# State-space decays from cumulative sums spread over partitions through DRAM and subtracted on GpSimd, experts taken in pairs, rotation prepared in halves

## The reference, cut to what matters

```python
dt = jax.nn.softplus(dt_raw + dt_bias)
a = jnp.exp(-jnp.exp(A_log) * dt)
Bh = jnp.repeat(_rms(Braw), HEADS_PER_GROUP, axis=2) + B_bias
Ch = jnp.repeat(_rms(Craw), HEADS_PER_GROUP, axis=2) + C_bias
phi = jnp.cumsum(dt, axis=1)[..., None] * rope_freqs
Bh = _rope(Bh, phi)
Ch = _rope(Ch, phi)
u = xh * dt[..., None]
...
h = a_t[..., None, None] * h + u_t[..., None] * b_t[:, :, None, :]
y = jnp.einsum('bhpn,bhn->bhp', h, c_t)
```

```python
hid = x @ w1[e].T            # 352 wide: gate and up
act = weight[:, e] * silu(hid[:, :176]) * hid[:, 176:]
y += act @ w2[e].T
```

## Time and profile before

| | us |
|---|---|
| median of 3 runs | 3548.45 (3546.27 to 3550.61) |
| the profiled execution's own time | 3546.08 |
| its span | 3543.8 |
| state-space loop, one pass (window 1244.60 to 1302.90) | 58.30 |
| DVE busy in that pass | 50.68 |
| PE busy in that pass | 46.95 |
| POOL busy in that pass | 13.82 |

### The profile page before, as it was taken

One profiled execution on the slowest core, in us unless ns is written; L12 is line 12 of the kernel. 1 busy time (PEld: TensorE's weight loads), 2 busy tenths in 40 slices (PEclk: granted clock), 3 DMA queues, 4 the chain that ended last, 5 costly groups with the idle time before them and its releaser, 6 DMA issues. The chain is left out here.

```text
span 3543.8 us, 63690 instructions
## 1 busy us (share of the span) xinstructions
PE 2886.8 (81%) x24052; PEld 2012.8 (57%) x24052; DVE 2235.7 (63%) x4757; ACT 1481.2 (42%) x3064; POOL 628.6 (18%) x990
## 2 busy tenths in 40 slices
PE   6777699977767878848996958979999996888687
PEld 3333488867645555525664434536565565777576
DVE  6999644432658888866655733257777774433764
ACT  4899511111454646343442122245555541332222
POOL 5222100000002222111110014112222212322100
PEclk8899799989977776769998978989999997999798
DMA  4999900000010000010001050000000003000000
GB/s 122 199 204 205 225 4 0 0 24 3 17 54 3 3 2 3 2 73 10 6 12 50 23 143 24 0 7 4 3 3 3 3 3 148 1 1 1 1 1 13
DMA packets 316791, 141.92 MB, mean 40 GB/s; under 512 B 296251, under 2 KB 306107, under 8 KB 312897
## 3 DMA queue, kind: packets, MB, share of 16 engines
q1 hardware_dynamic: 308356, 138.85, 16.4%
q10 hardware_dynamic: 8256, 0.52, 0.2%
HBM read 68.04 MB, written 3.15 MB: 20 GB/s over the span
## 5 line engine op out<-in xcount | busy, mean ns | idle before, releaser
L1251 ACT ACTIVATE l0x_pb<-l0x_ex,l0x_neg_max,l0x_q_scale 128x2048 uint16<-128x2048 f32 x128 | 267.2, 2088 | 35.3 <-POOL l0x_neg_max L1354 24.8
L1150 PE MATMUL l0x_s_ps<-l0x_kT,l0x_qT 128*128 128x512 bf16 x512 | 178.3, 440 | 78.8 <-DVE l0x_ex L1449 42.1
L1447 DVE TENSOR_SCALAR_CACHE_REDUCE l0x_ex<-l0x_s_ps 128x1024 f32<-128x1024 f32 x128 | 156.1, 1220 | 13.6 <-PE l0x_s_ps L1150 12.8
L1449 DVE TENSOR_SCALAR_CACHE_REDUCE l0x_ex<-l0x_s_ps 128x1024 f32<-128x1024 f32 x128 | 156.1, 1219 | 1.0 <-PE l0x_s_ps L1150 1.0
L1150 PEld LDWEIGHTS l0x_s_ps<-l0x_kT,l0x_qT 128*128 128x128 bf16 x512 | 33.5, 101 | 157.7 <-DVE l0x_ex L1449 106.3
L264 PE MATMUL l3x_bank<-l3x_w_kv_x,l3x_ctxT 128*128 128x512 f32 x256 | 117.4, 601 | 4.4 <-ACT l3x_ctx_q L765 3.7
L2230 PE MATMUL l1a_bank<-l1a_r,l1a_r 32*64 32x64 f32 x2048 | 73.1, 285 | 44.6 <-DVE l1a_r L2572 40.1
L2238 PEld LDWEIGHTS l1a_bank<-l1a_u,l1a_gm 64*64 64x64 f32 x2048 | 97.7, 197 | 17.8 <-issue 17.0
L2238 PE MATMUL l1a_bank<-l1a_u,l1a_gm 64*64 64x8 f32 x2048 | 100.4, 237 | 7.5 <-DVE l1a_gm L2591 7.3
L264 PE MATMUL l2f_bank<-l2f_w,l2f_ln_yT 128*128 128x352 f32 x256 | 105.6, 548 | 0.0
L1160 PEld LDWEIGHTS l0x_o_ps<-l0x_v,l0x_vT 128*128 128x128 f16 x2048 | 71.6, 99 | 56.5 <-DMA l0x_vT<-l0x_pb 26.7
(11 more groups left out here) (775 smaller groups left out, 7690.5 us busy)
## 6 DMA issues: line engine op xcount, KB each, us to landing
l2f_wproj_raw<-in_L_xattn_wproj SPq DMA_DIRECT2D x2, 2048.0 KB, 13.4
l3a_w<-in_L_attn_W SPq DMA_DIRECT2D x4, 1024.0 KB, 11.8
l2f_w<-in_L_ffn_w SPq DMA_DIRECT2D x1, 2816.0 KB, 10.7
l0x_ex<-in_ctxT SPq DMA_DIRECT2D x8, 256.0 KB, 5.3
l0a_wq<-in_L_attn_W_Q SPq DMA_DIRECT2D x1, 2048.0 KB, 11.4
l0a_wk<-in_L_attn_W_K SPq DMA_DIRECT2D x1, 2048.0 KB, 14.2
l0x_vT<-l0x_pb SPq DMA_TRANSPOSE x128, 4.7
l0a_wv<-in_L_attn_W_V SPq DMA_DIRECT2D x1, 2048.0 KB, 8.0
```

Source lines behind the costliest of these rows:

```text
L1150: ins = mm(s_ps[:, j * 512:(j + 1) * 512], qT[:, h, :], kT[:, h // 2, j * 512:(j + 1) * 512], start=True, stop=True)
L1251: s.activation(pb[:, h % 4, :], ex[:, h % 4, :], ACT.Exp, scale=q_scale[:, h:h + 1], bias=nb[:, h:h + 1], accum_out=sums[:, h:h + 1]).then ...
L1447: v.tensor_scalar(ex[:, h % 4, 0:1024], s_ps[:, 0:1024], 1.0, None, ALU.mult, ALU.max, accum_out=low_max[:, h:h + 1]).then_inc(o.up(scores ...
L1449: v.tensor_scalar(ex[:, h % 4, 1024:2048], s_ps[:, 1024:2048], 1.0, None, ALU.mult, ALU.max, accum_out=high_max[:, h:h + 1]).then_inc(o.up ...
```

## The change

In the state-space part:

- The running sums are also copied times -exp(A_log) to cum_a (ACT, heads on partitions), stored in DRAM, and read back eight times a tile, each time 16 heads of one sequence broadcast to the 64 partitions of that sequence, straight into the decay tile (8 transfers of 64 x 4 KB). PE turns cum_a once, ACT copies it to cum_s, tokens on partitions.
- POOL subtracts cum_s and adds a mask, in place, two instructions of 128x1024 for each of the four rounds (function differences). ACT takes the exponential in place from SBUF.
- The step tiles, their instructions on DVE and POOL, and the matmuls 2218 and 2219 go. So do the DVE instruction for dt times a and the setup of the two masks.
- The bias of the B states is added by POOL alone, in four instructions of 128x1024, the first half of head groups first.
- On ACT the bias of C and the sines go by halves: bias, sines, bias, sines.

In the expert part two experts share one activation tile of 352 columns, which is transposed in three pieces (128, 128, 96) and multiplied in three matmuls, in place of two and two for each expert. The second weight matrix is laid out for that.

```diff
+            for t in range(TILES):
+                sp.wait_ge(cum_a_ready.sem, cum_a_ready.value(t))
+                sp.dma_start(cum_dram[t].rearrange("b h s -> h b s"), cum_a[0:H, :].rearrange("h (b s) -> h b s", b=2)).then_inc(cum_stored.sem, 16)
+                sp.wait_ge(cum_stored.sem, cum_stored.value(t))
+                for r in range(4):
+                    if t and r % 2 == 0:
+                        sp.wait_ge(gm_ready.sem, gm_ready.value(t - 1, r // 2 + 1))
+                    for b in range(2):
+                        src = cum_dram[t, b, 16 * r:16 * r + 16, :].unsqueeze(0).broadcast_to([S, 16, S])
+                        sp.dma_start(decay[b * S:(b + 1) * S, 16 * r:16 * r + 16, :], src).then_inc(spread_loaded[r].sem, 16)
...
-            def differences(t, r):
-                steps_ready = (even_steps, odd_steps)[r % 2]
...
-                    mm(bank[4 + j][:], later[:].rearrange("p b s -> p (b s)"), same[:].rearrange("p h s -> p (h s)"), start=True, stop=False)
-                    ins = mm(bank[4 + j][:], after[:], flat(steps_[:, 8 * j:8 * j + 8, :]), start=False, stop=True)
...
+            def turn_sums(t):
+                pe.wait_ge(cum_a_ready.sem, cum_a_ready.value(t))
+                pe.sem_inc(L.order["pe"], 1)
+                nc.tensor.transpose(cum_s_bank, cum_a[0:H, :], env.ident[0:H, 0:H]).then_inc(cum_s_ps.sem, 1)
...
+                s.activation(cum_a[:], bank[2][:, 256:384], ACT.Copy, scale=a_neg[:]).then_inc(o.up(cum_a_ready), 1)
...
             def decays(o, r):
-                act.wait_ge(diff_ps.sem, diff_ps.value(o.t, r + 1))
-                for j in range(2):
-                    h = 16 * r + 8 * j
-                    s.activation(flat(decay[:, h:h + 8, :]), bank[4 + j][:], ACT.Exp).then_inc(o.up(exp_ready if j else None), 1)
+                act.wait_ge(diff_ready.sem, diff_ready.value(o.t, r + 1))
+                d = flat(decay[:, 16 * r:16 * r + 16, :])
+                s.activation(d, d, ACT.Exp).then_inc(o.up(exp_ready), 1)
...
+                    act.wait_ge(roped.sem, roped.value(t, 1))
+                    biased_c(o, 0)
+                    sums_out(o)
+                    sines(o, 0)
                     act.wait_ge(roped.sem, roped.value(t))
-                    biased_c(o)
-                    sines(o)
+                    biased_c(o, 1)
+                    sines(o, 1)
...
+            def differences(o, r):
+
+                heads = slice(16 * r, 16 * r + 16)
+                d = decay[:, heads, :]
+                pool.wait_ge(spread_loaded[r].sem, spread_loaded[r].value(o.t))
+                pool.wait_ge(cum_s_ready.sem, cum_s_ready.value(o.t))
+                g_.tensor_tensor(d, d, cum_s[:, heads].unsqueeze(2).broadcast_to([P, 16, S]), ALU.subtract).then_inc(o.up(), 1)
+                pool.wait_ge(o.sem, o.at())
+                g_.tensor_tensor(d, d, mask[:].unsqueeze(1).broadcast_to([P, 16, S]), ALU.add).then_inc(o.up(diff_ready), 1)
...
-                steps_of(o, 2)
...
-                    steps_of(o, 0)
-                    biased_b(o)
                     fractions(o)
...
+                for n, (a, w) in enumerate(self.parts):
+                    ins = nc.tensor.matmul(self.y, self.actT[0:w, pair % 2, n, :], self.w_out[0:w, pair, n, :],
+                                           start=(pair == 0 and n == 0), stop=(2 * pair == E - 2 and n == len(self.parts) - 1))
```

More of the change, by code:

```diff
@@ L599, in __init__ @@
         self.fixed, self.factor = fixed, factor
-        self.parts = [(a, min(P, inner - a)) for a in range(0, inner, P)]
+        self.parts = [(a, min(P, 2 * inner - a)) for a in range(0, 2 * inner, P)]
         self.score = L.sb(f"{name}_score", [P, 8])
@@ L665, in scalar @@
                 s.activation(self.sg[:, i % 2, :], self.hb[i % 2][:, 0:I], ACT.Silu).then_inc(o.up(self.silu), 1)
[L666 to L671, removed]
+            if i >= 2 and i % 2 == 0:
+                pair = i // 2 - 1
+                o.eng.wait_ge(self.actT_ps.sem, self.actT_ps.value(o.t, pair + 1))
+                whole_rows = len(self.parts) - 1
+                s.activation(flat(self.actT[:, pair % 2, 0:whole_rows, :]), self.tb[:, 0:whole_rows * P], ACT.Copy).then_inc(o.up(), 1)
+                w = self.parts[-1][1]
+                s.activation(self.actT[0:w, pair % 2, whole_rows, :], self.tb[0:w, whole_rows * P:(whole_rows + 1) * P], ACT.Copy).then_inc(o.up(self.actT_ready), 1)
     def vector(self, o):
@@ L2286, in tile @@
                     whole(norm.tensor(pe, t + 1, bank[7]))
-                for r in range(2, 4):
-                    pe.wait_ge(exp_ready.sem, exp_ready.value(t, r))
-                    differences(t, r)
-                    if more and r == 2:
-                        pe.wait_ge(norm.ready.sem, norm.ready.value(t + 1))
-                        project_in(*states)
+                    pe.wait_ge(norm.ready.sem, norm.ready.value(t + 1))
+                    project_in(*states)
                 pe.wait_ge(gm_ready.sem, gm_ready.value(t, 1))
@@ L2354, in x_out, with sums_out, biased_c @@
                 o.eng.wait_ge(x_taken.sem, o.at(x_taken))
-            def biased_c(o):
+            def sums_out(o):
+                act.wait_ge(cum_s_ps.sem, cum_s_ps.value(o.t))
+                s.activation(cum_s[:], cum_s_bank, ACT.Copy).then_inc(o.up(cum_s_ready), 1)
+            def biased_c(o, half):
                 for e, dst in enumerate((v1[1], v2[1])):
-                    for k in range(NG):
-                        last = e and k == NG - 1
+                    for k in range(half * NG // 2, (half + 1) * NG // 2):
+                        last = e and k == (half + 1) * NG // 2 - 1
@@ L2387, in _ @@
             states_out(first)
-            biased_c(first)
-            sines(first)
+            for half in range(2):
+                biased_c(first, half)
+                if half == 0:
+                    sums_out(first)
+                sines(first, half)
             x_out(first)
@@ L2456, in _ @@
             first = Order(pool, L.sem("pool_first_order"))
             norms(first)
-            pool.wait_ge(dt_ready.sem, dt_ready.value(0))
-            odd_steps_of(first, 1)
-            biased_b(first)
+            pool.wait_ge(mask_set.sem, mask_set.value())
+            for half in range(2):
+                biased_b(first, half)
+            for r in range(2):
+                differences(first, r)
             def tile(t, more):
@@ L2466, in tile @@
                     o.t = t
-                odd_steps_of(o, 3)
+                differences(o, 2)
+                differences(o, 3)
                 if more:
@@ L2470, in tile @@
                     scales_of_states(o)
-                    pool.wait_ge(dt_ready.sem, dt_ready.value(t + 1))
-                    odd_steps_of(o, 1)
-                    biased_b(o)
+                    for half in range(2):
+                        biased_b(o, half)
+                    differences(o, 0)
+                    differences(o, 1)
                     o.t = t
```

151 lines of the change are left out of this document (61 added, 90 removed).

## The result

The changed kernel takes **3573.4 us** (median of 4 runs, 3570.0 to 3578.7), the kernel before 3547.4 beside it (4 runs, 3545.9 to 3550.6). The ratio is 1.0074, 95% interval 1.0056 to 1.0091: slower by 26 us. The prediction said 3595, with 3565 to 3625 as its range. The profiled execution is the longest of the four, 3578.7 us with a span of 3576.9.

The account below looks back on a forecast made before the run. The prediction took the state-space pass to be bound by a chain on DVE. From 3546.1 us profiled, +66.4 for the state-space part and -18 for the experts gave 3594.5, stated as 3595, range 3565 to 3625.

Parts of the forecast that it names:

- They alternate: State-space part: POOL's differences and DVE instructions with two SBUF inputs take turns, a difference priced at 1.9 us.
- A: Behind the layer norm: four differences meet the rotation, DVE waits 7.2 us; +4.85 us, in 7 passes +34.0.
- B: End of the pass: differences of rounds 0 and 1 hold DVE 5.0 us; +3.6, in 7 passes +25.2.
- C: Ahead of the loop: rotation starts about 4.2 us earlier, but all four first differences fall in it; +2.4 us.
- last tile: Last tile of the state-space part: four differences cost 7.6 us, less old waits of 1.7 and 1.1; +4.8 us.
- POOL waiting for no transfer: End of the pass: a store and two loads fit in 7.3 us, so the DRAM trip costs nothing.
- I take -18 us; bounds -22 and -10: Experts on PE: 0.685 us saved a pair, 21.9 in all, less about 1 us at each of 4 round ends.
- 2.06 instead of 2.74 us: Experts on PE: forecast time of a pair's transposes and output matmuls on one tile, after instead of before.
- No blocking: Rival, state-space part: POOL's differences and the rotation run side by side, all waits fall out; 3494 us, chance 0.11.
- Late rows: Rival, end of the pass: store and loads exceed 7.3 us, four differences meet the rotation; +18, 3613 us, chance 0.15.
- DVE keeps its turn: Rival, state-space part: POOL waits until DVE's run of two-input instructions ends; some +40, 3568 us, chance 0.08.
- Experts give nothing: Rival, expert part: ACT or the hidden values' waits bind, so no gain; 3612 us, no chance of its own given.

Follow-up runs that it names:

- e6: The changed kernel without the 32 mask additions on GpSimd, four instructions a tile instead of eight: 3511.0 us, ratio 0.9894 to the kernel before.
- e7: The changed kernel with GpSimd's difference rounds 2 and 3 held until the second half's first rotation products end: 3560.1 us, ratio 1.0026 to the kernel before.
- e5: The changed kernel with the store and loads through DRAM in tile 0 alone: 3578.2 us, ratio 1.0079 to the kernel before.
- e1: The kernel before with only the expert part changed, state-space part as before: 3507.1 us, ratio 0.9891 to the kernel before.

## Why it came out so, step by step

**The waits of DVE and GpSimd on each other, right.** "They alternate", at 1.9 us a turn, is what the rows after show, and the sum holds at each place. A: +4.85 forecast, +5.23 measured (DVE held 7.4 for 7.2; line 233 takes 0.55 again). B: held 5.0 as forecast; from the first fraction to the next statistics 24.6 us became 28.4, +3.8 where 5.0 less the sine wait of 1.57 was forecast. Weigh comes 8.6 us ahead of the fractions for 8.3 (+0.3, as forecast). From the first weigh to the second a pass is 0.6 shorter, where 0.15 was forecast. C: from the first statistics to the second +3.3 for +2.4; the masks' setup was to give 0.6, and the first fraction came 0.4 later instead. Six passes: +9.0 each for +8.45, the first of them 68.4 us long. The last pass with the last tile: +13.3 for 8.45 + 4.8. In all +70.4 for +66.4. The pass was said to be 66.7 and is 67.0 to 67.2 from the second on. e6 and e7 show the cause by count and by place.

**What was costed at nothing, right.** The half biases on POOL lie under the fractions; PE's turned sums cost 0.3 us; the sine wait is gone in the loop. "POOL waiting for no transfer" was right from the second pass on; the two waits before it, 1.30 and 0.68 us, were not forecast, and e5 shows what the transfers cost: some 1 us.

**The experts, mis-sized.** The term that was off is "I take -18 us; bounds -22 and -10": it measured 43 us in the profile and 39 in e1, outside its bounds. The row behind it was read rightly (two output matmuls in 1.15 us). The error was in dividing it: "two output matmuls 1.15", so one is 0.575 and three are 1.73; three took 1.30. The interval belongs to the pair of neighbours, not to the instruction: 0.28 of the 1.15 stood at the edges of the 48-row piece, and 0.10 more in the projection behind. All of it goes when no piece has 64 rows or fewer. The other part of the term, some 4 us for PE's wait for ACT's copy at the end of each of four rounds, was too large: PE is idle for 0.31 us at each such place. "2.06 instead of 2.74 us" for a pair's transposes and output matmuls came out as 0.32 + 1.30 = 1.62. A finer view of before would have told it. In PE's timeline, in windows narrow enough to part the four records of line 655 (the count is that of the records in reach, the start is what counts):

```profile
2218.41 0.60 PE L655 MATMUL l2f_bank<-l2f_w,l2f_moe_actT 128*128 128x256 f32 x2
...
2218.63 0.79 PE L655 MATMUL l2f_bank<-l2f_w,l2f_moe_actT 128*128 128x256 f32 x2
...
2218.94 0.70 PE L655 MATMUL l2f_bank<-l2f_w,l2f_moe_actT 48*128 48x256 f32 x2
```

0.22 us from the first record to the second, 0.31 to the third, for the same 256 columns; the rest to 2219.56 is 0.31 for each of the two 48-row records.

**The total.** Against the profiled execution: 3594.5, less 25 for the experts, plus 4 for the state-space part and 6 for the parts that did not change, is 3579, and it took 3578.7. The median of the four is 5 lower. Medians compared, +26 us was measured where some +48 was forecast, and nearly all of the difference is the experts' term.

**The rivals.** No blocking (3494): out, by every row shown. Late rows (3613): out by e5, and by POOL's rows from the second pass on. DVE keeps its turn (3568): it names nearly the right time, and by a mechanism that the rows refute, since DVE and POOL change turns after each instruction. Experts give nothing: out by e1. A total that agrees with a rival says nothing for it; the stages do.

## What to carry to other kernels

Work moved to an idle GpSimd was free here only where it did not meet a DVE instruction with two SBUF tiles: put GpSimd's 128x1024 instructions beside DVE instructions that read PSUM, and price each one that meets a DVE instruction with two SBUF tiles at its own full length. When matrices are cut into pieces for PE beside matmuls of 128 rows, let no piece have 64 rows or fewer (88 and 88 or 104 and 72, not 128 and 48 or 112 and 64) before counting instructions; it is one small change, and gave 23 us here. And price a matmul from its start to the next start for each kind of neighbour, not as a share of a group.

## What the runs showed of the hardware

- Where the contraction changed from 128 or 112 rows to 48 or 64, and back, the weights were loaded only as the matmul started: two intervals of 0.10 us more at each such edge, 0.39 us an expert. With 72, 88, 96 and 104 rows the loads lay ahead, also next to 128 rows, and so they did between two records of 48 rows.
- POOL can also hold a DVE instruction with one SBUF tile. In e5 POOL's difference began 0.1 us earlier in the pass than in the kernel after, and it was line 213 (128x256, two values per partition from SBUF) that stood still for 1.7 us. DVE, then POOL:

```profile
1277.21 2.09 DVE L213 TENSOR_SCALAR l1a_ln_y<-x_stream,l1a_ln_mv,l1a_ln_rstd 128x256 f32 x1 [1.01 <-POOL l1a_ln_rstd L233]
```

```profile
1277.25 1.90 POOL L2459 TENSOR_TENSOR l1a_decay<-l1a_decay,l1a_cum_by_token 128x1024 f32<-128x1024 f32 x1 [0.16 <-POOL l1a_ln_rstd L233]
```

  The Trainium skill ("SBUF — State Buffer", section "Who interferes with whom") has tensor_scalar among the operations that can enter a mode that uses both ports, and so contend with GpSimd; this row agrees with it (2.09 for 0.41 us). Who asked first it doesn't show: DVE's is issued 0.04 us ahead, and it is DVE's that is held.

  The sum at that place stayed the same, 14.69 us from the statistics to weigh for 14.65: one more instruction was held in front and one fewer behind.
- The trip through DRAM, a store and the loads of 256 KB for rounds 0 and 1, fits under the 7.5 us of the bias from the second pass on, though a load's median is 6.1 us; in the first pass POOL waited 0.68 us for it.
